# Issuing the row-maximum products of the first head group earlier in a two-block attention kernel

## The reference

```python
xn1 = _ln(x, g1, be1)
q = jnp.einsum('btc,hcd->bhtd', xn1, Wq_s) + bq      # 16 heads of 32
k = jnp.einsum('bsc,hcd->bhsd', xn1, Wk_s) + bk
v = jnp.einsum('bsc,hcd->bhsd', xn1, Wv_s) + bv
scores = jnp.einsum('bhtd,bhsd->bhts', q, k) / scale
scores = jnp.where(mask[None, None], scores, -jnp.inf)
attn = jax.nn.softmax(scores, axis=-1)
out = jnp.einsum('bhts,bhsd->bhtd', attn, v)
x = x + (sa @ W1 + b1)
```

## Time and profile before

| | us |
|---|---|
| median of 3 runs | 2349.21 |
| lowest and highest run | 2340.73, 2351.22 |
| the profiled execution's own time | 2340.73 |
| its span in the profile | 2338.9 |
| PE busy | 2198.0 (94%) |
| DVE busy | 1410.1 (60%) |
| ACT busy | 868.2 (37%) |
| POOL busy | 933.6 (40%) |

### The profile page before, as it was taken

One profiled execution on the slowest core, in us unless ns is written; L12 is line 12 of the kernel. 1 busy time (PEld: TensorE's weight loads), 2 busy tenths in 40 slices (PEclk: granted clock), 3 DMA queues, 4 the chain that ended last, 5 costly groups with the idle time before them and its releaser, 6 DMA issues.

```text
span 2338.9 us, 31417 instructions
## 1 busy us (share of the span) xinstructions
PE 2198.0 (94%) x11206; PEld 1595.5 (68%) x11206; DVE 1410.1 (60%) x3349; ACT 868.2 (37%) x1598; POOL 933.6 (40%) x943
## 2 busy tenths in 40 slices
PE   7999999999999998789999998999999999999996
PEld 5655565556555654447777776788887887888784
DVE  5477757875786566735666668453455546454646
ACT  3155545654565455533443334321111122112213
POOL 1068657766777577773333333010111202011212
PEclk9999999999999998789999999999999999999998
DMA  7465545553556356212111121321112121212011
GB/s 231 55 93 97 92 71 77 103 93 62 83 97 97 60 88 124 69 56 85 59 55 55 59 95 55 113 86 36 50 54 75 52 82 44 87 55 68 33 36 50
DMA packets 106320, 177.29 MB, mean 76 GB/s; under 512 B 18334, under 2 KB 23454, under 8 KB 106160
## 3 DMA queue, kind: packets, MB, share of 16 engines
q1 hardware_dynamic: 106164, 175.29, 32.4%
HBM read 83.67 MB, written 40.13 MB: 53 GB/s over the span
## 4 chain that ended last, share of the span: by engine, by line
PE 75%; DVE 9%; issue 6%; ACT 4%; POOL 3%; DMA 2%; SPq 0%; POOLq 0%; ACTq 0%; DVEq 0%
PE psum L55 18%; PE psum L56 17%; PE psum L57 17%; PE psum L797 5%; PE psum L745 5%; PE psum L785 4%; PE psum L806 2%; DMA small<-es 2%; PE psum L703 1%; DVE psum L1000 1%; POOL es L660 1%; ACT sx L1346 1%; PE psum L1300 1%; DVE mx L1004 1%; PE psum L1292 1%
## 5 line engine op out<-in xcount | busy, mean ns | idle before, releaser
L660 POOL TENSOR_TENSOR es<-es,er 128x512 f32<-128x512 f32 (+3 forms) x640 | 589.6, 961 | 322.5 <-PE psum L797 283.4
L895 ACT ACTIVATE er<-psum 128x512 f32<-128x512 f32 (+3 forms) x640 | 280.4, 470 | 316.0 <-DVE psum L1011 181.2
L1000 DVE CUSTOM_DVE_ANT_0 psum<-psum,mask_ts 128x384 f32<-128x384 f32 (+3 forms) x512 | 247.9, 500 | 201.2 <-PE psum L745 200.5
L785 PE MATMUL psum<-qs,ks 100*128 100x512 f32 (+3 forms) x768 | 264.5, 377 | 17.1 <-DVE mx L1004 6.6
L745 PE MATMUL psum<-ks,qs 96*128 96x512 f32 (+3 forms) x768 | 267.2, 373 | 10.9 <-DVE mx L1000 6.6
L1850 ACT ACTIVATE fy<-psum,cols 128x512 f32<-128x512 f32 x128 | 88.2, 689 | 451.4 <-PE psum L57 450.9
L745 PEld LDWEIGHTS psum<-ks,qs 96*128 96x128 f32 x768 | 144.0, 194 | 109.7 <-issue 39.4
L1004 DVE TENSOR_REDUCE mx<-psum 128x1 fp32r<-128x512 f32 x256 | 175.1, 684 | 60.7 <-PE psum L745 59.8
L785 PEld LDWEIGHTS psum<-qs,ks 100*128 100x128 f32 x768 | 145.9, 196 | 92.4 <-DVE mx L1004 23.1
L55 PE MATMUL psum<-fh,hh 128*128 128x512 f32 x512 | 201.1, 393 | 7.1 <-DVE hl L1951 7.1
L55 PE MATMUL psum<-fah,fh 128*128 128x512 f32 x512 | 202.6, 396 | 0.0
(11 more groups left out here) (258 smaller groups left out, 4479.8 us busy)
## 6 DMA issues: line engine op xcount, KB each, us to landing
qs<-stage SPq DMA_DIRECT2D x96, 256.0 KB, 5.7
ks<-stage SPq DMA_DIRECT2D x96, 256.0 KB, 6.9
rs<-rs_d SPq DMA_DIRECT2D x32, 256.0 KB
sa_d<-rs SPq DMA_DIRECT2D x32, 256.0 KB, 2.2
sx<-sa_d SPq DMA_DIRECT2D x8, 1024.0 KB, 5.7
xt<-in_x SPq DMA_DIRECT2D x32, 256.0 KB, 6.1
x_d<-xt SPq DMA_DIRECT2D x32, 256.0 KB, 2.0
fw<-in_Wf SPq DMA_DIRECT2D x16, 512.0 KB, 5.3
```

The source lines that it names most:

```text
L660: e.tensor_tensor(es, es, er, ALU.add).then_inc(s_add.sem, 1)
L785: t = e.matmul(ps[:, off:512], Q.ks[par][0:100, i, 128 * j:128 * j + 128], Q.qs[par][0:100, i, 512 * c2 + off:512 * c2 + 512], start=True, ...
L895: e.activation(dst, bank1("sc", g, c2, j, i)[:, off:512], ACT.Exp, scale=SCALE).then_inc(s_freeS.sem, 1)
L1000: t = e.tensor_tensor_reduce(out=ps, in0=ps, in1=mask_ts[:, 512 - wd:512], scale=1.0, scalar=-3e38, op0=ALU.add, op1=ALU.max, accum_out=mx ...
```

## The change

One line of `order1` changes: the times at which the maximum steps of group 0 are laid out. For the first half they begin at 36 instead of 46 and end at 47 instead of 54; those of the second half begin where the first end, and their end stays where it was. `mxT`, `tq` and `tqd` of the first half follow at fixed distances behind the end of that half, and so move from 54 to 47 as well. The other groups' entries are the same.

```diff
-        m0, m1, end = (at0(46), at0(54), cut - 0.12) if g == 0 else (0.25, 0.5, 0.97) if g == 1 else (g - 1.02, g - 0.72, g)
+        m0, m1, end = (at0(36), at0(47), cut - 0.12) if g == 0 else (0.25, 0.5, 0.97) if g == 1 else (g - 1.02, g - 0.72, g)
         t += spread(m0, m1, max_steps(g, 0)) + spread(m1, end, max_steps(g, 1))
         for c2, at in enumerate((m1, end)):
             t += [(at + 0.04, ("mxT", g, c2)), (at + 0.06, ("tq", g, c2)), (at + 0.09, ("tqd", g, c2))]
```

## The result

| | before | after |
|---|---|---|
| median, us | 2348.81 (5 runs) | 2360.27 (5 runs) |
| lowest and highest | 2340.73, 2351.22 | 2355.35, 2362.05 |
| the profiled execution's own time | 2340.73 | 2361.88 |
| its span | 2338.9 | 2360.1 |

A forecast was written before the change was run, and what follows sets the result against it. PE was taken as the bound, one chain without idle time from 52 to 110 us. Wait 9.6 + clock 1.7 + second waits 0.5 - what comes back 0.5 = 11.3 us, on the median 2349.21 giving 2360.5, range 2349 to 2367.

The forecast's parts named there:

- When the operands land: Group 0's start: the third first-half k transfer, needed by the first maximum product, lands at 62.0 us.
- k would land 1.9 us earlier: Rival on k's first-half transfers: landing at 60.1, wait 7.7 us, total 2358.6 us; chance 0.11.
- The new wait: PE at the moved first maximum product: idle from 52.42 until k lands at 62.0, 9.6 us (7.7 to 9.6).
- The clock: PE's work behind the new wait: half clock for 3.4 us, losing 1.7 us, between 0 and 6.5.
- back some 4 us behind the gap: Sign in the changed profile: granted clock falls to 0.50 in PE's gap and returns some 4 us behind it.
- the last matmul of the second half's k projection: Sign on PE's timeline: it comes at about 71 us instead of 58.13.
- the clock stays low: Rival for PE's work behind the wait: clock low some 13 us, costing 6.5 us, total 2365.3 us; chance 0.13.
- Second waits: PE at second-half products r = 11 and r = 12: no transfer wait; 0.5 us for banks, bounds 0 to 2.
- What comes back: Behind 110 us: PE's 3.4 us of waits for maxima shrink, giving back 0.5 us, bounds 0 to 3.4.
- The sum: Whole kernel: 11.3 us slower, 2360.5 us on the median; first scores about 11 us later.

The follow-up runs named there:

- e8: The changed kernel itself, unaltered, measured once more beside other kernels: 2354.36 us (5 runs), ratio 1.0036.
- e4: Kernel before with only the start of the first half's maxima moved (36 to 54): 2359.42 us (5 runs), ratio 1.0052.
- e5: Kernel before with the first half's maxima from 40 to 47: 2354.27 us (6 runs), ratio 1.0030.
- e6: Kernel before with the first half's maxima from 43 to 51: 2356.11 us (5 runs), ratio 1.0038.
- e1: Kernel before, order kept, with PE made to wait for first-half q and k before the third second-half q projection step: 2362.02 us (5 runs), ratio 1.0064.
- e7: The change with two thin z products (6 and 7) moved behind the first step of v: 2358.23 us (5 runs), ratio 1.0043.
- e10: Kernel before with e1's added wait, and z products 6 and 7 moved behind the first step of v: 2357.89 us (8 runs), ratio 1.0045.
- e11: The change with z products 6 and 7 moved as in e7, a second look: 2358.94 us (one run).
- e2: The change with 36 unused matmuls put ahead of the first maximum product's wait, so PE works through the gap: 2354.77 us (8 runs), ratio 1.0032.
- e3: Kernel before with only the end of the first half's maxima moved (46 to 47): 2349.28 us (12 runs), ratio 1.0014.
- e9: Kernel before with the first half's maxima later, 50 to 58 instead of 46 to 54: 2345.4 us (11 runs), ratio 0.9988.

## Why the prediction was right, and where it was not

- *When the operands land:* 62.0 was read off; 60.8, 62.0, 61.6, 61.5 and 62.0 were measured (change, e8, e4, e5, e6). In the change's trace q's transfers were issued 0.9 us earlier than before (46.47 against 47.36), which accounts for 0.9 of the 1.2 us. That k would land 1.9 us earlier because later transfers are gone did not come true: they are worth 0.2 to 0.7 us. The Trainium skill, "DMA: Bandwidth & Descriptors", section "Queues, rings and completion order", says that completion is not first-in, first-out per issuing engine. For these transfers on one queue the traces show order: in e5 k's third lands at 61.5, and q's next two, issued behind it, at about 63.6 and 65.6.
- *The new wait:* forecast 9.6, measured 7.8 to 8.3 in the change, and 9.3 in e4. The mechanism, place and releaser are as written, and e1 shows that it is enough by itself. PE's arrival varies as well, from 52.4 (e4, e7) to 54.4 (e8), of which the fall of the clock at 51.4 in e8 makes 1.5. In the change's trace, too, the clock fell ahead of the stretch, with PE busy all the time:

```profile
46.00:48.00 2.00, 2.00 (x6) 1.58 (x5) 1.97 (x5) 1.05 (x2) 0.00 (x0) 0.50 0.79 292
```

- *The clock:* forecast 1.7, measured 7.6 and 4.8 behind the gap in the two traces of the change, and in the second another 1.5 ahead of it. This is the mis-sized term, and 7.6 lies above its upper bound too. That bound, 6.5 from the earlier trace rows, was the better row. I took the idle time nearest in length; what followed it there were 16 transposes in a row, and what follows here is broken up by thin products, which e7, e10 and e11 show to matter. The sign "back some 4 us behind the gap" failed: it was 15.2 and 9.7 us, and the last matmul of the second half's k projection ran at 74.77 instead of about 71. The rival "the clock stays low" described the change's trace; it had 0.13. The two `z` products of the earlier trace rows say nothing about the granted clock, which is recorded as 1.00 from 18 to 24 us, around the one of 5.67 us. The Trainium skill, "TensorE: Matmul & The Clock Gate", section "What's actually happening", says that activity releases the clock and idleness throttles it; the gap and e2 agree, and e6 shows the fall behind 3.69 us of idle time. The falls with PE busy all the time, as in the row above, it doesn't account for.
- *Second waits:* none at r = 11 or r = 12, as forecast, and PE waited for no bank in the stretch. The 0.5 us was not there. e3 shows what the term would look like with the products packed closer.
- *What comes back:* 3.4 - 2.6 = 0.8 us against 0.5. In the trace of e9, with later maxima, PE's waits in the same three rows are 4.1 + 0.9 + 0.9 = 5.9 us, and yet its median is no worse. Most of that is one wait, some 95 us behind the first scores, which is 1.3 to 1.6 us in ten of the thirteen traces and 3.8 to 4.1 in e1, e3 and e9. Whether the early maxima shorten it, which would explain part of why the change loses less than e1, no run separates from chance.
- *The sum:* to the first scores it should have been 11 and was 16.2 and 14.8. The medians moved by 11.5 us in the first comparison and by 11.2 with all executions together (2357.9 against 2346.7). That the forecast of 2360.5 fell on 2360.3 is partly luck: the first median of before, 2348.8, lies 2 us above the later ones, and the clock term was too small by 4.6 to 5.9 us where the wait was too long by 1.3 to 1.8. The start's delay (16.2 and 14.8 us) is larger than the loss that the ratios give (12.0 and 8.5), and where the 4 to 6 us between them go isn't shown, beyond the 0.7 us of products done sooner. The part behind the first scores varies by 10 us over the thirteen traces, and by 5 between the two of the changed kernel, which hides it.

## What to carry to other kernels

Before a step is moved ahead in an in-order queue, compare the moment at which its queue reaches the new place with the landing of what it waits for: here 52.4 against 61 to 62, where the old place had 3 us in hand and eight more would have cost nothing. A stall of PE has a second price, the work behind it at half clock, and in these traces that price depends on what stands behind the stall more than on its length: a stall of some 8 us cost 2.5 us more (e7) or 7.6 us more (the change), one of 3.7 us 4.6 more (e6). Read it from the traces of the same work, take the worst row as a serious case, and compare traces by stage, since executions of one kernel differ by as much as the change.

## What was unexpected of the hardware

- An idle time of 3.69 us was enough to bring the granted clock from 1.00 to 0.50 (e6), and the work behind ran at 1.2 GHz for 9.1 us. The fall of the earlier trace rows, in the kernel before, came within an even shorter one:

```profile
914.87 0.47 PE L745 MATMUL psum<-ks,qs 96*128 96x128 f32 x1 [1.98 <-DMA ks<-stage]
```

- The clock's return goes with what PE does: it came 2.8 to 5.1 us behind the gap where projections and maximum products alone followed (3 traces), and 8.6 to 15.2 us behind it with thin products among them (6 traces).
- The clock fell without idle time too, in e10 while thin products followed one another (0.71 and 0.50 from 70 to 74 us, PE busy 2.00 of 2), and in seven of the thirteen traces (the change, e1, e2, e3, e7, e9, e11) for 3.4 us between 44 and 50 us, among dense projections. The trace before is not one of them, and no run shows what decides it.
- 8.34 us of useless matmuls in place of idle time kept the clock at 1.00 and moved the first scores from 129.5 to 122.1 (e2).
